# Second attention: the scores of the second query tile as three products of rounded parts

## What is computed

```python
x = x + attn_a(layernorm(x));  x = x + ffn(layernorm(x))
# attn_b: 16 heads, a query of 128 + 64 features, latent keys of 64 + 64
q_nope, q_pe = split(x @ wq);  ckv, k_pe = split(x @ wkv_a)
ckv = rms_normalise(ckv) * kv_norm_scale
k_nope, v = split(ckv @ wkv_b)
q_pe, k_pe = rope(q_pe), rope(k_pe)
scores = (q @ k.T) * (128 + 64) ** -0.5, causal
x = x + softmax(scores) @ v @ wo
x = x + ffn(layernorm(x))
```

## Time and profile before

| | |
|---|---|
| median of 3 runs | 940.77 us (940.66 to 945.98) |
| the profiled execution | 944.91 us |
| its span, first to last instruction | 942.9 us |
| granted TensorE clock, mean | 0.971 |
| busy shares | PE 91%, DVE 76%, ACT 56%, POOL 46% |

### The profile page before, as it was taken

One profiled execution on the slowest core, in us unless ns is written; L12 is line 12 of the kernel. 1 busy time (PEld: TensorE's weight loads), 2 busy tenths in 40 slices (PEclk: granted clock), 3 DMA queues, 4 the chain that ended last, 5 costly groups with the idle time before them and its releaser, 6 DMA issues.

```text
span 942.9 us, 19230 instructions
## 1 busy us (share of the span) xinstructions
PE 856.5 (91%) x6286; PEld 649.1 (69%) x6286; DVE 717.7 (76%) x2366; ACT 531.3 (56%) x1392; POOL 434.7 (46%) x683
## 2 busy tenths in 40 slices
PE   6678898889999999987999999999999997999996
PEld 5556666667765666655888787887888775666663
DVE  6567988889778887663968787787868686888872
ACT  5356544454354555545676676757586761555555
POOL 0348898887766665446202121221202012556655
PEclk9779999999999999989999999999999999999999
DMA  6333333332223557102112020202021022234331
GB/s 211 60 50 49 53 56 55 56 55 38 35 37 58 103 118 133 43 14 46 24 24 46 1 46 1 45 2 46 2 45 37 11 35 35 36 71 59 59 48 35
DMA packets 49938, 46.55 MB, mean 49 GB/s; under 512 B 5280, under 2 KB 47280, under 8 KB 49840
## 3 DMA queue, kind: packets, MB, share of 16 engines
q1 hardware_dynamic: 49840, 45.33, 26.2%
HBM read 11.40 MB, written 2.10 MB: 14 GB/s over the span
## 4 chain that ended last, share of the span: by engine, by line
PE 33%; DVE 15%; issue 3%; ACT 1%; POOL 1%; DMA 0%; POOLq 0%; SPq 0%; DVEq 0%; ACTq 0%
PE bank L301 8%; PE bank L1979 6%; PE bank L1987 4%; PE bank L1913 4%; DVE weights L1476 3%; PE bank L1928 3%; DVE weights L1466 3%; PE bank L1743 2%; PE bank L1756 2%; DVE q_lo L1456 1%; PE bank L1739 1%; DVE rope L1454 1%; PE bank L1782 1%; DVE xn L338 1%; DVE arena L1313 1%
## 5 line engine op out<-in xcount | busy, mean ns | idle before, releaser
L1313 DVE TENSOR_REDUCE arena<-bank 128x2 f32<-128x512 f32 (+1 forms) x192 | 130.9, 685 | 42.4 <-PE bank L1743 41.4
L924 ACT ACTIVATE weights<-bank 128x512 f32<-128x512 f32 x144 | 85.8, 596 | 109.1 <-PE bank L1756 108.3
L1006 ACT ACTIVATE weights<-weights,neg_max 128x128 f32<-128x128 f32 (+1 forms) x256 | 113.9, 449 | 39.2 <-DVE neg_max L1466 38.7
L727 POOL TENSOR_SCALAR_AFFINE_SELECT weights<-weights 128x256 f32<-128x256 f32 x144 | 68.6, 478 | 101.4 <-ACT weights L924 101.4
L1979 PE MATMUL bank<-kbT,arena 128*128 128x128 f32 (+1 forms) x512 | 105.1, 328 | 1.0 <-DVE y L447 0.9
L667 POOL TENSOR_SCALAR weights<-weights 128x512 f32<-128x512 f32 x64 | 97.6, 1537 | 12.5 <-ACT weights L832 12.5
L1743 PE MATMUL bank<-kf_stack,q_stack 96*128 96x256 f32 (+1 forms) x256 | 99.7, 432 | 0.0
L1013 ACT ACTIVATE weights<-bank 128x384 f32<-128x384 f32 x128 | 62.7, 490 | 61.0 <-PE bank L1987 60.5
L1466 DVE CUSTOM_DVE_ANT_0 weights<-bank,arena 128x128 f32<-128x128 f32 (+1 forms) x256 | 80.2, 350 | 14.6 <-PE bank L1979 12.6
L301 PE MATMUL bank<-x_hi,wb_hi 128*128 128x256 f32 x256 | 83.8, 327 | 2.8 <-DVE q_lo L1456 2.8
L1476 DVE TENSOR_SCALAR weights<-weights,inv_sum 128x128 f32<-128x128 f32 (+1 forms) x256 | 81.3, 360 | 4.6
(11 more groups left out here) (236 smaller groups left out, 2514.2 us busy)
## 6 DMA issues: line engine op xcount, KB each, us to landing
q_stack<-q_hi SPq DMA_DIRECT2D x96, 128.0 KB, 4.5
arena<-arena SPq DMA_DIRECT2D x64, 128.0 KB, 2.5
q_stack<-q_lo SPq DMA_DIRECT2D x48, 128.0 KB, 5.3
ka_stack<-k_hi SPq DMA_DIRECT2D x32, 76.5 KB, 2.8
x_all<-x SPq DMA_DIRECT2D x8, 256.0 KB, 5.1
st_wo<-b_wo SPq DMA_DIRECT2D x8, 256.0 KB, 4.2
arena<-b_wqn SPq DMA_DIRECT2D x8, 256.0 KB, 3.3
out<-x_all SPq DMA_DIRECT2D x8, 256.0 KB, 2.1
```

Source lines behind the costliest of these rows:

```text
L924: a.activation(s["pT"][(STEPS * b + k) % N_PT], p2[k % 2][:, :], ACT.Exp).then_inc(s["exp"], 1)
L1006: last = a.activation(p, p, ACT.Exp, scale=-1.0, bias=neg_max[:, h % 4, t:t + 1], accum_out=sums[:, h % 4, t:t + 1])
L1313: v.tensor_reduce(into, p1[k % 2][:, :].rearrange("p (s g k) -> p s g k", s=n, g=NC), AX.X, ALU.max, negate=True).then_inc(s["maxed"], 1)
```

## The change

Attention b's batches 0 to 6 get their scores of query tile 1 (128 queries by 256 keys) from three fp32r products in place of one fp32 product; tile 0, and all of batch 7, stay as they were. The rounded and low parts are made in pairs of heads: ACT rounds two heads' queries (`round_q`) behind its copy of the probabilities at every even slot h, for the heads h + 4 and h + 5; POOL subtracts (`low_q`) at the same slot, ahead of its part of `step_b`. The keys' parts are made at slot 8 (ACT, ahead of kbT) and slot 9 (POOL). The parts live in q_stack 0 and 1, which attention f leaves free in that time. `low_oT` moves from h % 4 == 1 to 2, `project_b` from h % 4 == 2 to 3, the residual from slot 3 to 4.

```diff
+        qr_hi, qr_lo = ([q_stack[0][:, lo + i, :].rearrange("p (h q) -> p h q", h=2) for i in range(2)] for lo in (2, 4))
+        kr_hi, kr_lo = ([q_stack[1][:, 4 * i + lo:4 * i + lo + 2, :] for i in range(2)] for lo in (0, 2))
...
+            if s is sf[1] and b == 0:
+                sp.wait_ge(*at(sm, "scores", B - 1, 0))
...
                     g.tensor_copy(kv_tok[par][:, :, W_ABS:], kv_tok[par][:, :, 0:LORA]).then_inc(sm["k_odd"], 1)
+                if h == 9 and b < B - 1:
+                    pool.wait_ge(*at(sm, "k_round", b, 1))
+                    pool.wait_ge(*at(sm, "kT", b, 1))
+                    g.tensor_tensor(kr_lo[par], kbT[par][:, :, :], kr_hi[par].bitcast(f32), ALU.subtract)\
+                        .then_inc(sm["k_rest"], 1)
...
+            def low_q(b, p):
+                pool.wait_ge(*at(sm, "q_round", b, p + 1))
+                g.tensor_tensor(qr_lo[p % 2], qT[b % 2][:, 2 * p:2 * p + 2, P:T], qr_hi[p % 2].bitcast(f32),
+                                ALU.subtract).then_inc(sm["q_rest"], 1)
...
+            for p in range(2):
+                low_q(0, p)
             for b in range(B):
                 for h in range(H):
+                    if h % 2 == 0 and b + (h + 4) // H < B - 1:
+                        low_q(b + (h + 4) // H, (h + 4) % H // 2)
                     if b + 1 < B:
                         step_b(b + 1, 1 - b % 2, h)
...
                 if h == 8:
                     act.wait_ge(*at(sm, "kT_ps", b, 1))
+                    if b < B - 1:
+                        if b == 0:
+                            act.wait_ge(*at(sf[0], "sT_ps", B - 3, STEPS))
+                        a.activation(kr_hi[par], halves(ps_a), ACT.Copy, scale=-SCALE_B).then_inc(sm["k_round"], 1)
...
+            def round_q(b, p):
+                if p == 0:
+                    act.wait_ge(*at(sm, "q_got", b, 128))
+                if p % 2 == 0:
+                    act.wait_ge(*at(sm, "qa_out", b, p // 2 + 1))
+                if (b, p) == (0, 0):
+                    act.wait_ge(*at(sf[0], "sT_ps", B - 1, STEPS))
+                act.wait_ge(*at(sm, "scores", b, 2 * p - 2))
+                a.activation(qr_hi[p % 2], qT[b % 2][:, 2 * p:2 * p + 2, P:T], ACT.Copy).then_inc(sm["q_round"], 1)
...
                     copy_probs(b, h)
+                    if h % 2 == 0 and b + (h + 4) // H < B - 1:
+                        round_q(b + (h + 4) // H, (h + 4) % H // 2)
                     if h % 4 == 0 and h > 0:
                         act_ctx(b, h // 4 - 1)
...
-                    if h == 1 and b > 0:
+                    if h == 2 and b > 0:
                         low_oT(b - 1, QUADS - 1)
-                    elif h % 4 == 1 and h > 1:
+                    elif h % 4 == 2 and h > 2:
                         low_oT(b, h // 4 - 1)
-                    if h == 3 and b > 0:
+                    if h == 4 and b > 0:
                         residual_b(b - 1)
...
+                mm(ps_s[h % 2][:, 0:P], qT[b % 2][:, h, 0:P], kbT[b % 2][:, h % 2, 0:P], start=True, stop=True)
+                if h == 0:
+                    pe.wait_ge(*at(sm, "k_rest", b, 1))
+                if h % 2 == 0:
+                    pe.wait_ge(*at(sm, "q_rest", b, h // 2 + 1))
+                parts = ((qr_hi, kr_hi), (qr_hi, kr_lo), (qr_lo, kr_hi))
+                for i, (q, k) in enumerate(parts):
+                    last = mm(ps_s[h % 2][:, P:P + T], q[h // 2 % 2][:, h % 2, :], k[b % 2][:, h % 2, :],
+                              start=i == 0, stop=i == 2, skip_group_check=True)
                 last.then_inc(sm["scores"], 1)
...
-                    elif h % 4 == 2:
+                    elif h % 4 == 3:
                         after_quad(b, h // 4 - 1, project_b)
```

More of the change, by code:

```diff
@@ L161, in hybrid_layers_kernel @@
                      qr_dve=4, qr_out=4, q_got=128, normed=2 * H, wo_ps=QUADS, scores=H, maxed=H,
-                     exp=H, pT_ps=H, copied=H, oT=QUADS, oT_lo=QUADS, o_ps=QUADS)
+                     exp=H, pT_ps=H, copied=H, oT=QUADS, oT_lo=QUADS, o_ps=QUADS,
+                     q_round=H // 2, q_rest=H // 2, k_round=1, k_rest=1)
         def at(s, name, b, n):
@@ L1021, in _ @@
                         round_mvo(k - 2)
+            for p in range(2):
+                round_q(0, p)
             exps_b(0, 0)
@@ L1977, in scores_b @@
                 pe.wait_ge(*at(sm, "maxed", b, h - 1))
-                for t in range(NT):
-                    last = mm(ps_s[h % 2][:, t * P:t * P + (t + 1) * P], qT[b % 2][:, h, t * P:(t + 1) * P],
-                              kbT[b % 2][:, h % 2, 0:(t + 1) * P], start=True, stop=True)
+                if b == B - 1:
+                    for t in range(NT):
+                        last = mm(ps_s[h % 2][:, t * P:t * P + (t + 1) * P], qT[b % 2][:, h, t * P:(t + 1) * P],
+                                  kbT[b % 2][:, h % 2, 0:(t + 1) * P], start=True, stop=True)
+                    last.then_inc(sm["scores"], 1)
+                    return
+                mm(ps_s[h % 2][:, 0:P], qT[b % 2][:, h, 0:P], kbT[b % 2][:, h % 2, 0:P], start=True, stop=True)
[7 more added lines that the diff above has]
+                              start=i == 0, stop=i == 2, skip_group_check=True)
                 last.then_inc(sm["scores"], 1)
```

## The result

The changed kernel takes **1010.99 us** (median of 4, 1010.11 to 1012.33); the kernel before, run beside it, 940.97 (median of 4, 940.66 to 945.98). The ratio is **1.0726** (95% interval 1.0703 to 1.075): slower, as forecast, but 27 us above the 984 predicted, and above the top of the range. The profiled execution took 1010.11 us, its span is 1008.1, the mean granted clock 0.954.

A forecast was written before the change was run, and what follows sets the result against it. It took DVE to bound slots 3 to 7 of the second attention and PE the others; 2.3 + 4.0 - 0.4 = 5.9 us a batch, times seven, plus 1.7 at the start gave +43, so 984 us, range 955 to 1000.

The forecast's parts named there:

- Slot 6: DVE waits for POOL's rotation 1, queued behind a low part that needs ACT's rounding: +4.0 us a batch, bounds 3.5 to 4.5.
- rival 2: Products win because POOL finishes rotation 1 before head 6's normalisation ends, so DVE never waits: 933 us, chance 0.06.
- Products and start: Three rounded products for one fp32 product save 0.4 us a batch; the first low part costs 1.7 once at the start.
- the 0.58 named as a sign: Heads' scores taking 0.58 us instead of 0.66 would show the products' predicted saving right.
- bound of 1.3 a batch: Upper bound on the products' saving, 1.3 us a batch, if PE set the end in every slot.
- DVE, in order, can do nothing: Slot 6: DVE stalls 4.0 us; rotation 2, low sum, head 8's maxima and head 7's normalisation queue behind.
- Slots 4 and 5: Rotation 1 late behind rms and low part (1.6), plus the moved projection: +2.3 us a batch, bounds 1.6 to 2.6.
- up to 1.0 more: Extra us a batch because the moved projection stands on PE ahead of rotation 0 and slot 4's work.
- They cost nothing: The keys' rounding and subtraction in slots 8 and 9 are covered by idle time; uncovered, 1.9 us a batch.
- rival 3: Port shared by DVE and POOL: four more collisions of 0.48 us a batch on normalisations; 997 us, chance 0.09.
- The forecast's own range: Range given for the main forecast without the rivals: 966 to 995 us, chance 0.73.

The follow-up runs named there:

- e11: Changed kernel plus unread identity products on PE, five in slot 6 ahead of the transposes and eight in slot 7 ahead of the projection: 998.77 us.
- e12: Changed kernel with POOL's old work of slot 4 (rms) done ahead of that slot's low part: 1007.34 us.
- e1: Changed kernel with POOL's low parts a slot later, at odd slots, behind POOL's part of step_b: 965.99 us.
- e5: As e1, but with low sum, residual and projection back in the slots of the kernel before: 952.78 us.
- e7: Kernel before plus the new products, nothing moved; parts made only for the first four heads and first two batches' keys, then reused: 942.88 us.
- e4: Changed kernel, moves included, with parts made only for the first four heads and first two batches' keys, then reused: 955.64 us.
- e2: Kernel before with only the moves: low sum, residual and projection a slot later: 957.66 us.
- e6: e5 with ACT's roundings a slot earlier, at odd slots, and POOL's low parts at even slots behind step_b: 951.1 us.
- e9: e5 without POOL's subtractions after the first four heads and two batches' keys; ACT's roundings stay and PE waits for them: 948.44 us.
- e3: Changed kernel plus eight unread identity products on PE in slot 7 ahead of the projection: 1005.23 us.
- e10: e5 without ACT's roundings after the first four heads and two batches' keys; POOL still subtracts, from stale rounded parts: 949.33 us.

## Why the prediction was wrong in size and right in direction

The loss is 1011.0 - 942.6 = 68 us. The first three rows are taken from the changed kernel (the first from its waits, not from a run), the others run by run. "A batch" is the difference in the mean time from one copy of kva_tok to the next: 52.17 in the changed kernel, 50.18 in e11, 51.70 in e12, 45.42 in e1, 43.92 in e5, 42.50 in e7, 42.95 before.

| step | us | a batch | from |
|---|---|---|---|
| DVE waits for rotation 1 | 28.7 | 4.1 | the waits after |
| half clock behind that stall | 12.2 | 2.0 | changed kernel to e11 |
| rms behind the low part | 3.6 | 0.5 | changed kernel to e12 |
| the moves, queue mended | 13.2 | 1.5 | e1 to e5 |
| roundings and subtractions in good places | 9.9 | 1.4 | e5 to e7 |
| products and start | 0.3 | -0.45 | e7 to before |

The first three add up to 44.5; e1, which mends all three at once, gained 45.0.

- **Slot 6, right.** "+4.0 a batch": 4.1, by the links named. It decides, as rival 2 said it would, and rival 2 fell with it.
- **Products and start, right.** 0.4 a batch against 0.45; 1.7 against 1.6; a head's scores take 0.57 of e7's chain of waits (0.22 at 557.21 and 0.35) for the 0.58 named as a sign. Of the bound of 1.3 a batch two thirds went nowhere, which fits slots that belong to round trips between engines; slot by slot that was not tried.
- **The step that failed first: the loop was priced as a delay alone.** The sum stops at "DVE, in order, can do nothing" and lists who stands behind it. It did not ask what PE does meanwhile and at what clock it comes back. PE idles 2.54 us in slot 6 and 3.37 in slot 7, and then goes through 3.4 to 6.8 us at 1.2 GHz once or twice a batch: 12 us that stand in no term and no rival.
- **"Slots 4 and 5", a sum near the truth by the wrong parts.** I put 1.6 on rms behind the low part and 0.7 on the moved projection. By the runs rms is worth 0.5 and the moves 1.4 to 1.65 (e4 against e7, e1 against e5, e2 against before) where nothing hides them. The error: I looked at slot 2 alone, and priced the uncovered wait there by the gap to one normalisation (1.2; it was 0.64 in e2). The projection covered PE in slot 14 as well, and there the whole round trip through ACT and DVE comes to light. And "up to 1.0 more" for rotation 0 behind the projection was 1.4, by the wait of 9.5 us in 7.
- **"They cost nothing", wrong.** The load of ACT and POOL was judged by their idle time, and a cover was named only for the keys' two in slots 8 and 9. Measured: 9.9 us in e5 (1.4 a batch), 8.2 in e6. ACT's idle time isn't free where its work lies between two engines that wait for it, as in e9.
- **The port, rival 3: the kind is right, the form is not.** I had left the collisions out of the sum and had them as four of 0.48 on normalisations; the 0.48 was read as the price of one POOL instruction, but two stand beside that pair (584.59 to 586.06). They come fewer and dearer (in a steady batch two slow normalisations, 2.01 and 1.07, where the kernel before has three of 1.03), and also on other instructions than the normalisations: the key's norm in the changed kernel, a k_rot product in e5, which is 0.55 a batch there. As a share of the 68 us they were not measured alone.

The forecast's own range, 966 to 995, is 3 us wider at each end than its bounds add up to (969 to 992). The half clock alone would have made 996 of the 984, still inside the full range; with the 9.9 of the load it is 1006, outside. With all terms at their measured sizes, the loop, the clock, rms, the moves, the load and the products, a batch grows by 4.1 + 2.0 + 0.5 + 1.5 + 1.4 - 0.45 = 9.05 us, of the 9.2 that the copies of kva_tok show; the split among them holds for this order of the runs, since moves and loop overlap. No version tried beats the kernel before. The products are faster, but by 3 us in all, and no arrangement of their parts was found that costs less than 8 (e6).

## What to carry to other kernels

When a wait closes a loop through an in-order engine, price two things: the loop, and what TensorE does during it, for if it runs dry the clock can fall, as it did here, and the work behind the stall then takes longer (2.93 us for 1.42). A block of TensorE work that seems to stand anywhere may be the cover of a round trip through other engines; before moving it, list every place where it stands and what would wait there without it. And before speeding up an operation, run it with its preparation left out: had that ceiling been known (ratio 1.0), nothing else needed to be built.

## What the runs showed of the hardware

- **The clock.** PE's timeline of the changed kernel, the first product behind each of the two gaps; the clock falls in the second gap, at 571.5:

```profile
566.43 0.55 PE L2040 MATMUL bank<-cst,weights 128*128 128x128 f32 x3 [2.54 <-DVE weights L1517]
...
572.33 0.58 PE L1969 MATMUL bank<-q_stack,oT_hi 128*128 128x256 f32 x1 [3.37 <-DVE q_stack L1524]
```

 Steps between products are 0.21 us behind them, 0.12 at full clock (2.93 and 1.42 for twelve). With products in both gaps the clock stays at 1.00 (e11), with them in the second alone it is 0.97 (e3). The Trainium skill (TensorE: Matmul & The Clock Gate, HAM oscillation — how this bites in real kernels) tells of TensorE falling back to half clock at every step of a loop in which it waits for DMA; the trace agrees, with a wait for VectorE in each batch in DMA's place.

- **VectorE beside GpSimd.** The key's norm, two instructions of 64 columns, took 0.47 as a pair in the kernel before, where POOL did nothing beside it; in the changed kernel it meets POOL's rotation 0 and takes three times that. DVE's timeline before:

```profile
586.92 0.47 DVE L1444 SCALAR_TENSOR_TENSOR kv_tok<-kva_tok,rms,norm_bc 128x64 f32<-128x64 f32 x2
```

POOL's timeline after:

```profile
562.28 0.74 POOL L769 TENSOR_TENSOR arena<-rope,q_lo 128x256 f32<-128x256 f32 x1
562.98 0.73 POOL L770 TENSOR_TENSOR arena<-rope,q_lo 128x256 f32<-128x256 f32 x1
```

and DVE's timeline:

```profile
562.35 1.44 DVE L1485 SCALAR_TENSOR_TENSOR kv_tok<-kva_tok,rms,norm_bc 128x64 f32<-128x64 f32 x2 [0.26 <-POOL rms L755]
```

 A VectorE instruction of 0.2 us can thus cost 0.75, about as long as POOL's instruction beside it. A pair meets two of POOL's: here it ends with the second of them (563.79 and 563.71), and in e10 with the first low part behind the keys' subtraction (560.33, and about 560.2). So the price of a collision follows POOL's durations. The Trainium skill (SBUF — State Buffer, SBUF: two separate sides) has the port they share as a lock held for a whole instruction, and these rows agree with that. One overlap shows no delay: at 561.80 DVE's sum of the k_rot products into kv_tok takes 0.29, as in the kernel before, while POOL's rms of two columns is on record from 561.63 to 562.32, and so in five more batches; no run here says why.
